# A layer norm in two pieces on VectorE: where its centring and its normalising stand among the attention steps

## What is computed

```python
Q = (img_embed @ Wq).reshape(B, -1, H, D).transpose(0, 2, 1, 3)     # B=8, 256 rows, H=8, D=256
K = (sent_embed @ Wk).reshape(B, -1, H, D).transpose(0, 2, 1, 3)    # sent_embed: 256 rows of 192
V = (sent_embed @ Wv).reshape(B, -1, H, D).transpose(0, 2, 1, 3)
score = jnp.einsum('bhqd,bhkd->bhqk', Q, K) / math.sqrt(D)
score = jnp.where(mask, score, -jnp.inf)
attn = jax.nn.softmax(score, axis=-1)
ctx = jnp.einsum('bhqk,bhkd->bqhd', attn, V).reshape(B, -1, H * D)
out = ctx @ Wo + img_embed
mu, var = jnp.mean(out, axis=-1, keepdims=True), jnp.var(out, axis=-1, keepdims=True)
return (out - mu) * jax.lax.rsqrt(var + EPS) * gamma + beta
```

## Time and profile before

| | before |
|---|---|
| median of 3 runs | 322.97 us (322.92 to 323.16) |
| the profiled execution, its own time | 323.15 us |
| its span, first to last instruction | 321.3 us |
| PE busy | 314.5 us, 98% of the span |
| DVE busy | 253.1 us, 79% |
| ACT busy | 221.9 us, 69% |
| POOL busy | 181.1 us, 56% |
| granted TensorE clock | 1.00 in every stretch read |

### The profile page before, as it was taken

The page is one execution under the profiler, slowest core; times in us unless marked ns, Lnnn a source line. Parts: engine busy times, 40 slices in busy tenths (PEclk is TensorE's granted clock), DMA queues, the critical chain, the costliest instruction groups (busy, mean ns, idle before and its releaser), DMA issues.

```text
span 321.3 us, 8037 instructions
## 1 busy us (share of the span) xinstructions
PE 314.5 (98%) x2574; PEld 308.1 (96%) x2574; DVE 253.1 (79%) x721; ACT 221.9 (69%) x601; POOL 181.1 (56%) x183
## 2 busy tenths in 40 slices
PE   8999999999999999999999999999999999999993
PEld 7998888999999999999999999999999999999992
DVE  0466878778998889977997799977997799975686
ACT  2446677678777797668767787768766887767640
POOL 1122476558855586548755686457845686447311
PEclk9999999999999999999999999999999999999999
DMA  7995453453444545364356435354257435440001
GB/s 255 369 406 204 135 166 130 139 197 133 135 128 161 191 150 165 132 201 149 114 186 198 149 94 187 125 205 155 104 170 207 168 82 171 162 134 0 35 0 65
DMA packets 46911, 50.27 MB, mean 156 GB/s; under 512 B 3504, under 2 KB 37040, under 8 KB 46896
## 3 DMA queue, kind: packets, MB, share of 16 engines
q1 hardware_dynamic: 46608, 49.56, 46.1%
q10 hardware_dynamic: 288, 0.52, 0.7%
HBM read 32.24 MB, written 17.83 MB: 156 GB/s over the span
## 4 chain that ended last, share of the span: by engine, by line
PE 95%; DMA 2%; DVE 1%; SPq 1%; POOLq 0%; issue 0%; POOL 0%
PE score_bank L328 24%; PE out_bank L328 19%; PE gL_bank L328 14%; PE tL_bank L328 14%; PE tU_bank L328 9%; PE gU_bank L328 7%; DMA wq_raw<-in_wqT 2%; PE spare_bank L328 1%; PE spare_bank L362 1%; PE tL_bank L362 1%; PE tL_bank L344 1%; PE tU_bank L344 1%; PE out_bank L368 1%; PE tU_bank L368 1%; PE out_bank L344 0%; PE spare_bank L344 0%
## 5 line engine op out<-in xcount | busy, mean ns | idle before, releaser
L1033 POOL TENSOR_TENSOR probs<-probs,inv_sum 128x512 f32<-128x512 f32 x64 | 66.6, 1041 | 88.1 <-DVE inv_sum L819 87.5
L628 ACT ACTIVATE probs<-neg_scores,neg_max 128x256 f32<-128x256 f32 x128 | 64.2, 502 | 32.7 <-DVE neg_max L808 32.7
L1056 POOL TENSOR_TENSOR pT_lo<-pT_raw,pT_hi 128x512 fp32r<-128x512 f32 x60 | 76.5, 1295 | 8.6 <-ACT pT_hi L584 8.6
L808 DVE CUSTOM_DVE_ANT_0 neg_scores<-score_bank,mask_bias 128x256 f32<-128x256 f32 x128 | 49.2, 421 | 6.2 <-PE score_bank L328 3.7
L584 ACT ACTIVATE tL_hi<-tL_bank 128x512 fp32r<-128x512 f32 x31 | 18.6, 599 | 38.0 <-PE tL_bank L328 38.0
L829 DVE STREAM_TRANSPOSE squares<-probs 128x512 f32<-128x512 f32 x60 | 42.3, 706 | 0.6 <-DMA scratch<-squares 0.4
L754 DVE TENSOR_TENSOR tL_lo<-tL_bank,tL_hi 128x512 fp32r<-128x512 f32 x31 | 21.4, 689 | 22.7 <-ACT tL_hi L584 22.6
L328 PE MATMUL gL_bank<-xT_hi,A_hi 128*128 128x256 f32 x128 | 35.6, 278 | 0.0
L328 PE MATMUL gL_bank<-xT_lo,A_hi 128*128 128x256 f32 x128 | 35.6, 278 | 0.0
L328 PE MATMUL gL_bank<-xT_hi,A_lo 128*128 128x256 f32 x128 | 35.6, 278 | 0.0
L584 ACT ACTIVATE pT_hi<-pT_raw 128x512 fp32r<-128x512 f32 x60 | 34.3, 623 | 0.0
(11 more groups left out here) (176 smaller groups left out, 1007.2 us busy)
## 6 DMA issues: line engine op xcount, KB each, us to landing
scratch<-squares SPq DMA_DIRECT2D x30, 512.0 KB, 2.6
pT_raw<-scratch SPq DMA_DIRECT2D x120, 128.0 KB, 3.1
xT_raw<-in_xT SPq DMA_DIRECT2D x8, 256.0 KB, 3.6
ctxT_raw<-in_ctxT SPq DMA_DIRECT2D x8, 256.0 KB, 3.8
wo_raw<-in_wo SPq DMA_DIRECT2D x4, 512.0 KB, 13.6
x_res<-in_x SPq DMA_DIRECT2D x8, 256.0 KB, 3.2
out<-y SPq DMA_DIRECT2D x7, 256.0 KB, 2.5
wq_raw<-in_wqT SPq DMA_DIRECT2D x3, 512.0 KB, 7.8
```

What stands on the lines that cost most here:

```text
L628: nc.scalar.activation(probs[j % 2][:, n, :], neg_scores[:, n, :], ACT.Exp, bias=neg_max[:, n:n + 1], scale=-1.0, accum_out=row_sum[:, n:n ...
L808: nc.vector.tensor_tensor_reduce(out=neg_scores[:, n, :], in0=score_bank[hh][:, q, :], in1=mask_bias[:], scale=-SCALE, scalar=3.0e38, op0= ...
L1033: nc.gpsimd.tensor_tensor(probs[j % 2][:, rows, :], probs[j % 2][:, rows, :], inv, ALU.mult) \
L1056: nc.gpsimd.tensor_tensor(pT_lo[j % 2][:, k].rearrange("p hh (q i r) -> p (hh q) i r", q=QT, i=ROWS), pT_raw[j % 2][:, k].rearrange("p i n ...
```

## The change

`centre(ends)` moves within the step j = 0 from behind `transpose_squares(t, j, 0)` to behind `transpose_squares(t, j, 1)`, that is behind the low parts of gU and gL. `normalise(ends)` moves from the end of step j = 0 to the end of step j = 1, and the loop gives that step its `ends`. The other engines' code is untouched.

```diff
@@ -926,14 +926,14 @@
                 if by_squares:
                     transpose_squares(t, j, 0)
-                if ends is not None and j == 0:
-                    centre(ends)
                 gU_lo_part(t + 1, 0)
                 gU_lo_part(t + 1, 1)
                 gL_lo_part(t + 1)
                 if by_squares:
                     transpose_squares(t, j, 1)
                 if ends is not None and j == 0:
+                    centre(ends)
+                if ends is not None and j == 1:
                     normalise(ends)
                 if ends is not None and j == 3:
                     add_residual(ends)
@@ -961,7 +961,7 @@
                 step(PAIRS * b + 4, 0, b + 1, ends=b - 1)
-                step(PAIRS * b + 5, 1, b + 1)
+                step(PAIRS * b + 5, 1, b + 1, ends=b - 1)
             step(STEPS - 2, 2, B - 1)
```

## The result

| | before | after |
|---|---|---|
| median of 4 runs beside each other, us | 323.07 (322.92 to 323.20) | 327.92 (327.42 to 329.94) |
| profiled execution, us (its span) | 323.15 (321.3) | 329.94 (328.1) |

The changed kernel is slower: 1.0166 times the kernel before (1.0128 to 1.0203; by the medians above 1.015). Run again in a later batch it gave 327.83 us (327.07 to 330.85, 6 runs). The ratios in this document leave out runs that lie over 1.5% above the fastest of their kernel, so they need not be the quotient of the medians, and none is given for the batch whose kernel before stands at 323.04 us: three of its 12 runs took 315.3 to 315.8 us, ratios would be against those three alone (1.024 to 1.042), and medians over all 12 are compared there.

The account below looks back on a forecast made before the run. It took PE as the bound, busy 314.5 of 321.3 us and waiting for nobody in the loop. Window waits of 1.8, 2.0 and 3.5 us gave 7.3, less 0.7 for landing: 6.6 us more, 329.6 us (324.0 to 331.5).

Parts of the forecast that it names:

- Part 1: Centring moved behind gL and the second transpose in step j = 0: cost and gain 0.
- Part 2: Normalising at the end of step j = 1, on DVE itself: nearly covered by 1.35 us idle time, nothing for PE.
- Part 3, (a) to (f): Lateness passed from normalising through SP, DMA and DVE to PE, in steps 17 and 18: PE waits 0.98 us.
- (b): Length of the normalising pair on DVE beside POOL: held until 176.30, bounds 0.95 and 2.02 us, upper end taken.
- (c) to (e): Store of y issued at 176.40, squares' store 2.51 us behind, landing 4.21 us later; DVE 2.76 us late.
- Step 11: Window from step 9's loads: DVE's transpose at 112.23 instead of 109.04, PE waits 1.8 us with gL.
- Step 29: Last window, without loads: squares' store there by 294, ScalarE wants it at 294.91; cost 0.
- The mask's wait: Mask issued at 178.4, landing at 181.8 instead of ahead of 179.73; ends before the squares' wait, adds nothing.
- The windows behind steps 13 and 25: Squares' store landing in 5.00 us (4.99 in step 25), extra 0.79 all to PE: 1.77 us each, 3.5 together.
- B: Rival: no long hold, DVE's normalising pair takes 0.95 us; PE waits sum to 2.2 us, 325.2 us; chance 0.16.
- C: Rival: slack holds everywhere, faster landing at some 3.5 us and a short hold, PE never waits; 323.0 us; chance 0.12.
- D: Rival: hold and slow landings plus loads late for ScalarE, another 0.8 us per window; 333 us; chance 0.04.

Follow-up runs that it names:

- centre_only: Against the kernel before, only centring moves, behind gL's low part and the second transpose; normalising follows it, still in step j = 0: 323.65 us beside 322.95.
- store_behind: The changed kernel with SP issuing the next loads and the squares' store ahead of the store of y: 322.53 us beside 322.95 for the kernel before.
- after_again: The changed kernel run once more, unaltered, in a later batch: 327.83 us, beside 323.04 for the kernel before.
- beta_psum: The changed kernel with beta read from PSUM when normalising, one SBUF input less: 324.52 us, beside 327.83 for the changed kernel.
- loads_first: The changed kernel with the three loads issued ahead of the store of y, the squares' store still behind it: 322.61 us beside 322.95 for the kernel before.
- pe_pause: The kernel before with PE made to wait for ScalarE about a microsecond at each loop step entering j = 2: 327.06 us beside 323.31.
- normalise_only: Against the kernel before, only normalising moves, to the end of step j = 1; centring stays where it was: 327.06 us beside 323.04.
- beta_store_behind: The changed kernel with loads and squares' store ahead of the store of y, and beta in PSUM: 315.22 us beside 323.31 for the kernel before.
- affine_psum_old: The kernel before, order unchanged, with the loop's gamma and beta held in a PSUM bank: 315.34 us beside 323.09.

## Why the prediction was right, and where it was not

It forecast 329.6 us (324.0 to 331.5) and slower with 0.88; the median was 327.9.

**What bounds the kernel.** "In the loop PE waits for nobody" was wrong, by 0.03 us at one load, and this was the dearest of all waits. "So work that leaves another engine frees nothing" fell with it: 0.5 us taken off VectorE ahead of step 9 is worth 7.7 us. The slack was read from step 19, at 118 ns, where it is 2.06 and 1.81 us; in step 9, at 113 ns, the slack on gL was nothing. It was the wrong place to read it for the whole loop.

**Part 1** (centring, cost 0) was right in its size by accident. It does take centring from ahead of gL_lo in step 9, and the wait there is gone. But the held pair makes tU_lo late instead: in `centre_only` the spacing changes at 100.8, and in the changed kernel and in `store_behind` at 109.1 and 108.5, where tU_lo ends 0.05 us ahead of a load of the output (in the changed kernel 109.08 and 109.14) that comes 0.11 us late. One wait took the place of another, 0.7 to 1.6 steps later; that is 0.2 to 0.5 us.

**Part 2** was right: VectorE's own work cost nothing (`store_behind`).

**Part 3, (a) to (f).** (b) forecast 2.02 us for the pair, from two holds of 0.3 us; it was 1.88, by the branch that the text gave second (VectorE gets in first, POOL slips, the second instruction is held). (c) to (e): the store of y was forecast for 176.40 and issued at 178.88, with PE 2.62 us later at step 18 than before, so 176.26 against PE. The squares' store was forecast 2.51 behind it (2.50 measured), and 4.21 to land (4.19). In step 19 this gave 0.58 + 0.26 = 0.84 us for PE against the 0.98 forecast. Step 11: 1.95 against 1.8. Step 29 cost nothing, as said. The mask's wait is there (1.79 us) and ends before the squares' does, as said. It takes most of the idle time, though: one of the signs named, waits of 2 to 3 us of VectorE's squares for scratch, came as 0.9 us at most (0.89 behind the mask's 1.79).

**The windows behind steps 13 and 25** were mis-sized: 1.77 us each was forecast, since the store had taken 5.0 us there, and it was 0.86 and 0.78. All five landings took 4.1 to 4.5 us. What the forecast feared does occur: in `after_again` the store behind step 25 took 5.1 us, and PE lost 1.84 us there. The window behind step 21 cost 2.26 us instead of 0.98. The two steps ahead of it ran at 8.61 us, so that PE came earlier to its load, with VectorE the later of the two, and the store took 0.3 us longer than in step 17. The sum came out right, 6.7 us against 7.3 less 0.7, partly because these errors cancel.

**What the sum lacked** is the spacing. The change to 118 ns comes 14 us later than before (0.5 us), and the wait at 187 us brought 113 ns back until another short wait at 219.0 (3.5 steps, 1.2 us). That is the 1.7 us given back, and the size of the 1.7 us by which the median is under the forecast. In the other direction goes the fall of the granted clock behind a wait of 2 us, which is in the one profiled execution. The runs of 330.68 and 330.85 us in the later batch may have it too: their mean granted clock is 0.993 and 0.992, and 0.996 to 0.999 in the other four. But a run of 327.67 us has 0.990, and none of these three has a trace.

**The rivals.** B (no long hold, 325.2) fell by the 1.88 us; `beta_psum`, which takes the hold away, is the case that it describes, and measured 324.5: 1.7 us of waits where B had 2.2, less 0.7 us since the spacing changes two steps later than before. C (the slack holds everywhere) fell for the order as it stands, since the three loads take the DMA with the store, as its "against" said; with them out of the way the store lands in 2.9 us, and C comes true in `loads_first`. D had no part.

**Open.** Why a wait changes the spacing of the loads, and to which value. In `pe_pause` it was the other one six times out of six. In the changed kernel, where a second wait (gL_lo) follows on the first, the five windows began at 118 ns and left it at 118 four times and at 113 once; in `after_again` three times and twice. In `normalise_only` the spacing changed in three of the five windows, once to 118 and twice to 113. What tells these cases apart isn't known. Of 12 runs of the kernel before in one batch, three took 315.3 to 315.8 us, the time of the kernels without a change of spacing; that a margin of 0.03 us sometimes falls the other way fits, but none of the three has a trace. In the other batches all runs of it but one (629 us) lay at 322.8 to 323.8.

## What to carry to other kernels

A wait of one engine's work in a shared DMA queue is priced by what stands between it and the next transfer that someone needs: count the issues behind it and the traffic that they put ahead of that transfer, and try the loads ahead of the wait. Read the slack of a deadline at every repetition, the first ones above all, and from the starts and ends themselves, for a wait of 0.03 us is in no list. Where two engines exclude each other at SBUF, moving one operand to PSUM can be worth more than moving the instruction.

## What the runs showed of the hardware

- PE's weight loads (fp32r, 128x256 moving) come at one of two spacings, 113 or 118 ns, at a granted clock of 1.00 in both: 8.61 or 8.95 us a step; a kernel that stays at 113 takes 315.3 us, the one that changes at 94.91 takes 323.1. In one trace each of six equal pauses of PE changed it to the other (`pe_pause`); it changed at waits of 0.03 us as well (before, and the changed kernel at 219.0), and with no wait in the loop it stayed at 113 (`beta_store_behind`, `affine_psum_old`).
- VectorE's layer norm instruction with two SBUF inputs, beside POOL's pT_lo, is held until POOL's is through: 1.52 instead of 0.48 us. Where VectorE gets in first, POOL's pair grows by 0.24 us (2.79 and 2.55). With one of the inputs in PSUM neither happens (0.83 us a pair).
- The squares' store (128x1024, 512 KB) lands in 2.6 us alone, 2.9 behind the store of y, and 4.1 to 4.5 behind the store of y and three loads in the changed kernel (5.1 once in `after_again`).
- Behind a gap of 2.1 us between two loads of PE the granted clock was 0.66 on average over the next 4.5 us (a mix of 1.2 and 2.4 GHz), which cost 1.5 us, in one execution. The other gaps in that execution (0.6 to 1.8 us) and in `after_again` (up to 1.9 us) show a clock of 1.00 behind them.
